# Expert blocks: the down product of the preceding block in two halves of rows, behind the fifth and the seventh gate chunk

## What is computed

```python
def step(acc, p):                      # for each of 8 experts, F = 816
    uw, ub, gw, gb, dw, db, w = p      # w: weight of the token for this expert, 0 for most
    h = silu((xf @ gw.T + gb) * (xf @ uw.T + ub))
    return (acc + w[:, None] * (h @ dw.T + db), None)
```

## Time and profile before

| | us |
|---|---|
| median of 3 runs | 1214.55 (1212.95 to 1215.14) |
| profiled execution | 1211.91 |
| its span | 1210.0 |
| PE busy in the span | 1059.1 (88%) |
| DVE busy | 845.9 (70%) |
| ACT busy | 835.8 (69%) |
| POOL busy | 710.9 (59%) |
| granted clock of PE, mean | 0.961 of full speed |

### The profile page before, as it was taken

One profiled execution on the slowest core, in us unless ns is written; L12 is line 12 of the kernel. 1 busy time (PEld: TensorE's weight loads), 2 busy tenths in 40 slices (PEclk: granted clock), 3 DMA queues, 4 the chain that ended last, 5 costly groups with the idle time before them and its releaser, 6 DMA issues.

```text
span 1210.0 us, 29293 instructions
## 1 busy us (share of the span) xinstructions
PE 1059.1 (88%) x8776; PEld 969.8 (80%) x8776; DVE 845.9 (70%) x1946; ACT 835.8 (69%) x1988; POOL 710.9 (59%) x959
## 2 busy tenths in 40 slices
PE   2877889898999898989899999999999999999940
PEld 2556778787878787868899999998999999999940
DVE  4375466566656566566888888888888888888725
ACT  5565567676767676864777777777777777777810
POOL 5343646262727272641677777778777777777730
PEclk9888899999999999999999999999999999999975
DMA  9790011010101000312411111155211421144129
GB/s 328 248 274 14 24 58 48 26 48 26 52 22 52 22 30 22 147 54 103 158 34 35 35 35 35 34 176 191 69 35 35 149 87 35 35 142 155 40 94 323
DMA packets 63731, 106.73 MB, mean 88 GB/s; under 512 B 8333, under 2 KB 51342, under 8 KB 62032
## 3 DMA queue, kind: packets, MB, share of 16 engines
q1 hardware_dynamic: 56096, 86.55, 22.3%
q0 software_dynamic: 7600, 19.74, 4.6%
HBM read 138.52 MB, written 37.50 MB: 145 GB/s over the span
## 4 chain that ended last, share of the span: by engine, by line
PE 26%; ACT 23%; DVE 20%; issue 14%; SPq 2%; DVEq 1%; DMA 1%; POOL 1%; ACTq 0%; POOLq 0%
DVE gu_s L1168 6%; PE bank L1249 6%; DVE gu_s L1175 6%; ACT hf L834 5%; PE bank L1251 5%; PE bank L1250 5%; DVE hf L1188 3%; ACT gs L827 3%; DVE ys L1204 2%; PE bank L1342 2%; ACT gu_s L845 2%; PE bank L1380 2%; PE bank L1373 2%; ACT ht L838 2%; PE bank L1352 2%
## 5 line engine op out<-in xcount | busy, mean ns | idle before, releaser
L1249 PE MATMUL bank<-xt_h,gu_s 128*128 128x256 f32 (+1 forms) x1014 | 293.0, 289 | 22.6 <-DVE hf L1188 20.2
L1250 PE MATMUL bank<-xt_l,gu_s 128*128 128x256 f32 (+1 forms) x1014 | 287.3, 283 | 0.0
L1251 PE MATMUL bank<-xt_h,gu_s 128*128 128x256 f32 (+1 forms) x1014 | 286.8, 283 | 0.0
L649 POOL TENSOR_TENSOR ht<-hf,ht 128x256 fp32r<-128x256 f32 (+1 forms) x273 | 242.7, 901 | 64.6 <-ACT ht L838 54.9
L1175 DVE TENSOR_TENSOR gu_s<-raw_gu,gu_s 128x512 fp32r<-128x512 f32 (+1 forms) x273 | 203.7, 768 | 64.0 <-ACT gu_s L845 63.9
L1249 PEld LDWEIGHTS bank<-xt_h,gu_s 128*128 128x128 f32 (+1 forms) x1014 | 192.1, 189 | 29.6 <-issue 26.8
L1251 PEld LDWEIGHTS bank<-xt_h,gu_s 128*128 128x128 f32 (+1 forms) x1014 | 192.2, 190 | 0.0
L1250 PEld LDWEIGHTS bank<-xt_l,gu_s 128*128 128x128 f32 (+1 forms) x1014 | 191.7, 189 | 0.0
L834 ACT ACTIVATE hf<-hf 128x256 f32<-128x256 f32 (+1 forms) x273 | 113.4, 415 | 83.6 <-DVE hf L1188 77.5
L738 ACT ACTIVATE sm<-sm,least 128x256 f32<-128x256 f32 x256 | 127.4, 501 | 35.0 <-DVE least L1024 34.9
L640 POOL TENSOR_TENSOR dw_s<-raw_dw,dw_s 128x256 fp32r<-128x256 f32 x117 | 109.3, 960 | 68.4 <-ACT dw_s L852 67.7
(11 more groups left out here) (182 smaller groups left out, 2720.5 us busy)
## 6 DMA issues: line engine op xcount, KB each, us to landing
raw_gu<-in_gu_dram SPq DMA_DIRECT2D x39, 1648.0 KB
raw_dw<-in_dw_dram SPq DMA_DIRECT2D x39, 768.0 KB
xs_dram<-zrec SPq DMA_DIRECT2D x6, 1677.0 KB, 18.4
xr<-xs_dram SPq DMA_DIRECT2D x39, 258.0 KB, 2.8
yg<-y_dram SPq DMA_DIRECT2D x16, 512.0 KB, 8.2
xwin<-xt_dram SPq DMA_DIRECT2D x8, 640.0 KB, 4.2
raw_dw<-in_dw_dram SPq DMA_DIRECT2D x78, 64.0 KB
xg<-in_x_dram SPq DMA_DIRECT2D x8, 512.0 KB, 7.4
```

The lines of the kernel that those rows point to most:

```text
L649: nc.gpsimd.tensor_tensor(low, hf[0:m, ring(c), :], ht[0:m, p, 0, c, :].bitcast(F32), ALU.subtract).then_inc(h_split, 1)
L1249: nc.tensor.matmul(dst, lhs[0], rhs[0], start=start, stop=False)
L1250: nc.tensor.matmul(dst, lhs[0], rhs[1], start=False, stop=False)
L1251: return nc.tensor.matmul(dst, lhs[1], rhs[0], start=False, stop=stop)
```

## The change

PE alone is changed, in the expert blocks. `down(b, p)` becomes `down(b, p, t)` with t = 0 or 1 for one half of the rows. In block b the half t = 0 of block b - 1 is issued behind chunk 4 (the fifth, ROWS_AT = 4) and the half t = 1 behind chunk 6 (the seventh). The four waits that stood before the whole now stand before t = 0 (`down_ready`), and `y_full` rises after t = 1. The last block's two halves run one after the other at the end.

```diff
                     if c == ROWS_AT - 1 and (not isinstance(b, int) or b < NB - 1):
                         turn_rows(b + 1, 1 - p)
-
-            def down(b, p):
+                    if c == ROWS_AT and (not isinstance(b, int) or b >= 1):
+                        down(b - 1, 1 - p, 0)
+
+            def down(b, p, t):
+                if t == 0:
+                    down_ready(b, p)
+                for c in range(FCH - 1):
+                    passes(bank[5 + p][:, t * D:(t + 1) * D], [ht[:, p, i, c, t * P:(t + 1) * P] for i in range(2)],
+                           [dw_s[:, p, i, c * D:(c + 1) * D] for i in range(2)], c == 0, False)
+                for i in range(2):
+                    ins = nc.tensor.matmul(bank[5 + p][:, t * D:(t + 1) * D], ht[:, p, 0, FCH - 1, t * P:(t + 1) * P],
+                                           dw_s[:, p, i, DWW - D:DWW], start=False, stop=i == 1)
+                if t == 1:
+                    ins.then_inc(y_full, 1)
+
+            def down_ready(b, p):
                 pe.wait_ge(dw_split, b * DV + DV)
                 pe.wait_ge(dw_split_pool, b * (FCH - DV) + (FCH - DV))
                 pe.wait_ge(h_split, b * FCH + FCH)
                 if not isinstance(b, int) or b >= 2:
                     pe.wait_ge(y_ready, b - 1)
-                for t in range(2):
-                    for c in range(FCH - 1):
...
-                ins.then_inc(y_full, 1)
 
             def body(b, p):
                 gate_up(b, p)
                 if not isinstance(b, int) or b >= 1:
-                    down(b - 1, 1 - p)
+                    down(b - 1, 1 - p, 1)
             turn_rows(0, 0)
             blocks_of(pe, body)
-            down(NB - 1, (NB - 1) % 2)
+            for t in range(2):
+                down(NB - 1, (NB - 1) % 2, t)
```

## The result

| | before | after |
|---|---|---|
| median of the runs, us | 1214.44 | 1266.53 (1263.58 to 1267.42) |
| ratio | | 1.0427, 95% interval 1.041 to 1.0445 |
| profiled execution, us | 1211.91 | 1267.22 |
| its span | 1210.0 | 1265.4 |
| PE busy in the span | 1059.1 | 1065.3 |

The medians are over 4 runs each. One execution of a kernel further down, the kernel before with the early weight copy, took 1414.82 us at a mean granted clock of 0.697, where its six others had 0.954 to 0.962, and the ratios leave it out.

A forecast was written before the change was run, and what follows sets the result against it. The prediction took a ring of ScalarE and DVE, without PE, to bound the kernel. 50.8 + 4 - 2.5 = +52.3 us on 1211.91 gave 1264.2, plus 2.6 to the median 1266.8; forecast 1266, range 1240 to 1300 us (66% for 1250 to 1275).

The forecast's parts named there:

- The ring of ScalarE and DVE: Expert blocks: the two engines wait for each other and set the 15.12 us period; PE hangs on it at its fourth chunk.
- the three distances: DVE's first product to ScalarE's sixth bias 6.61 us, to DVE's low part 3.92, to the next first product 4.59.
- Slack of 0.99 us: Sixth gate chunk: its bias on ScalarE could have started at 813.81 and started at 814.80.
- +1.41 us per block: Sixth chunk ends 2.40 us later against 0.99 us of slack; ScalarE's bias and everything to the next block come later.
- steps 4 and 5: Seventh chunk hidden with 0.5 us to spare, down's second half with 4 us; moved half's operands ready with 3.3 us margin.
- Ends, +4 us: Blocks 1 and 38 also have the inserted half; between 0 and 2.40 us each, taken as 2 each.
- What comes back, -2.5 us: Slower blocks, where POOL waits for sends and then works beside DVE: of 4.9 us excess, 2.5 us vanish.
- Rival A, the clock: PE's clock falls behind its 1.77 us idle time: +20 us in a third of 36 blocks, +61 in all; 18%.
- The last step, the 2.6 us: The median of the runs lies 2.6 us above the profiled execution: 1264.2 becomes 1266.8 us.
- Rival B, faster: If PE were the bound, its wait at the fourth chunk would go: at most 16.8 us, 1198 us; 3%.
- Rival C: DVE's and POOL's slow-downs of each other shrink, saving 0.5 us per block of the 4.59 us tail: 1248 us; 7%.
- D: The moved half stalls on an operand and holds PE's queue; each us beyond the 3.3 us margin costs 37 us; 3%.

The follow-up runs named there:

- the kernel before with the early weight copy: Kernel before, with ScalarE's first of three next-block weight copies moved from behind the last SiLU to behind the second chunk's bias: 1197.83 us against 1213.32, ratio 0.9881.
- the second profile: The changed kernel executed once more, with no further edit: 1262.63 us, none of blocks 2 to 37 at the lower clock.

## Why the prediction held

- **What bounds the kernel.** The ring of ScalarE and DVE was read right: the early weight copy, which touches only that ring, shortened the kernel before. That the three distances add up to 15.12 us proves less than the prediction makes of it, since distances from one event to the next always add up to the period. What carries the reading is that no engine in it waits for anything but the step before. PE's own work was put at 14.76 us, and the experiment shows at most 14.65: subtracting the profile's idle time of 0.36 us leaves out about 0.1 us. It played no part in the sum.
- **Slack of 0.99 us.** Held: free at 0.72 us, 0.43 us of loss at 1.44 us, so 1.01. For the seventh chunk, 1.52 us of slack gave the wait of 0.88 us that was worked out from it.
- **+1.41 us per block.** Measured 1.37. The 0.04 us is DVE's tail, 4.55 instead of 4.59 us.
- **Covers that were named.** PE waited nowhere before the moved half, the seventh chunk and the second half stayed hidden, as steps 4 and 5 had it.
- **Ends, +4 us.** Block 1 +2.2 and block 38 +1.8 us: held.
- **What comes back, -2.5 us.** Mis-sized: -4.5 us. POOL still waits for its sends to land (10.9 us in 6 blocks, 10.0 in 6 before), but only 0.5 us of the excess is left. The excess over 35 blocks falls as the period grows: 519.80 - 35 x 14.65 = 7.1 us in the kernel before with the early copy, 4.9 us at 15.12, 1.8 us at 15.51, 0.8 us at 15.94, 0.5 us at 16.49. That the time which the ring gives POOL swallows its lateness fits this row and was not tested by itself.
- **Rival A, the clock.** The sum had it at zero, and it was there in the profiled run, with 6.2 us. This and the term before err in opposite directions, +6.2 and -2.0. The blocks gave 1.5 us less than 50.8, the last down product, whose clock was lower, 0.3 us more, and the 1.6 us before the stage and -1.6 us behind it cancel. So the profiled execution was forecast 3.0 us too low, 1264.2 against 1267.22. The last step, the 2.6 us from there to the median, was mis-sized too, since the median is 0.7 us below the profiled execution, and it took the 3.0 us back. So the 0.5 us between forecast and median is luck: the parts were good to some 5 us. In the second profile the clock's part is absent, and the time is 1262.63 us. The Trainium skill (TensorE: Matmul & The Clock Gate, A second HAM failure mode) tells of a clock that goes down and up again with frequent short idles between groups of matmuls. The traces agree for the longer ones here, at 2.45 us in two blocks of three, and not for idle times of 0.36 to 1.28 us in every block.
- **Rival B, faster.** Its condition, 2.40 us of slack, wasn't there. The rule of the Trainium skill (Perfetto Trace Analysis, Optimization Strategy) to look for the gaps on the busiest engine and for what ends them did lead to the right semaphore: PE's gap ended with DVE's product. The cure lay further round the ring, on ScalarE.
- **Rival C** did not happen in normal blocks (0.04 us), and **D** not at all.

## What to carry to other kernels

Follow the steps from an event to the same event one iteration later, and go on only along engines that are busy or wait for the step before. Where such a chain closes without the busiest engine, that engine only follows, and filling its gap is worth nothing as long as the chain stands. The sum of the distances alone proves nothing, because it is the period for any choice of events. Before moving work ahead of a result, read how late its reader really comes (no bracket before the reader's line means slack, and the start-to-start distance tells how much): up to that amount the move is free, beyond it every iteration pays in full. An in-order queue hands a wait on to all that stands behind it, so look first whether something behind the wait could run ahead of it.

## What the runs showed of the hardware

The granted clock doesn't follow from the length of an idle time alone. Idle times of 2.45 us, the same in every block, were followed by the lower of the two levels (1.2 instead of 2.4 GHz) in two blocks of three, in a fixed pattern, and idle times of 1.74 us in four blocks of 36 in one run and in none in another. What decides it stays open. Each time it costs some 1.5 us here (18.04 against 16.49, 18.75 and 18.65 against 17.20, 20.42 against the 18.89 of the sum): the slow stretch lies right behind the idle time, on the chunks that the ring waits for.
